# A two-layer decoder: layer norms from sums of the writing operation, squares on ScalarE, centred memory values, and a new order of the steps

## The chip, the cores and the metric

The kernel runs on one core of one Trainium2 chip. The metric is the time of one execution on the device in microseconds (us). One launch computes everything; the four sequences of the batch are worked off one after another, two at a time in flight.

## The reference, cut to what matters

Four sequences of 512 tokens with 256 channels, in float32, go through six sublayers. Each is added to its input and followed by a layer norm without weights:

```
x = LN(x + causal_attention(x))
x = LN(x + cross_attention(x, ctx, mask))   # its output goes through a norm of its own, gamma, beta
x = LN(x + sign_ffn(x))                     # three dense layers, weights +1 / -1
x = LN(x + performer(x))                    # linear attention, 16 heads, relu features
x = LN(x + mlstm(x, ctx, ctx))              # 8 heads, gated scores, norm of each head's 32 channels
x = LN(x + quantized_ffn(x))                # rounded tokens and weights, convolution, silu
```

The matrix LSTM of the fifth line, for each head: `H = (C @ v) / (max(|sum C|, exp(-m)) + 1e-6)`, then `(H - mean(H)) / sqrt(var(H) + 1e-5)` over the 32 channels of the head. `C` are scores times a decay, `v` the head's columns of ctx.

## The kernel before, in words

A sequence is worked on in two halves. The **front half** (names self, cross, sign, perf) holds the first four sublayers, the **back half** (first, mlstm, quant) the norm behind the performer and the last two. The back half of sequence b runs beside the front half of sequence b+1; the front half of sequence 0 and the back half of sequence 3 have nothing beside them. Each half has four PSUM banks, used in turn; a bank's next matmul waits until its last content was read.

Tokens lie on partitions in four tiles of 128, t = 0 to 3; "p" is a pair of tiles. There is no loop over engines: each engine has one queue in order, and its program for a half is a list of named steps (`yield "cross.score0"`). `weave` (L340) merges the lists of both halves, and of the preparation of weights (`prep`), by a table of due times (`FRONT_TIMES`, `BACK_TIMES`, `PREP_TIMES`, one column for each engine). The times decide nothing but the order in each queue: the step that is due first comes next, and an engine waits for every operand of it before it looks at the one behind.

The steps that matter here:

- **A layer norm** is `stats` (VectorE, L1351: `bn_stats` for each of two tiles, `bn_aggr` for each, one small addition), `rstd` (GpSimd, a power of -0.5), and `normalize` (VectorE makes the shift and tile 2p, ScalarE makes tile 2p+1). TensorE then turns the pair (`to_channels`, L806 to L812). There are six for a sequence and a seventh within the cross attention (`cross.in_`): 14 pairs for each sequence.
- **keep_clock** (L800) is a row of idle 128x512 matmuls that only keep TensorE busy: in front of `mlstm.cols` six of them (12 for the last sequence), and some in the performer and in the last half.
- **mlstm**: `gate`, `logf`, `csum`, `g`, `high`, `nmd`, `part2`, `part3` make the gates on VectorE one after another; `softplus`, `negated`, `part1` are ScalarE's share; `raw0`, `raw1` are the scores; `cols` turns the gates into columns, behind which GpSimd weighs the keys; `head0` to `head7` make the decay (matmul, exp on ScalarE, product on VectorE); then `out0` to `out3`. For each out tile VectorE does `ratio` and `square` (denominator in four small operations, the quotient L1758, its mean L1763, its centring L1765, gn_w L1769), ScalarE the squares (L2137), VectorE `var`, GpSimd a power (`pow`, L2276), VectorE `scale` (L1786, L1790).
- **quant**: `q0` to `q7` on VectorE (L1887, L1880) and ScalarE make the rounded hidden tiles; `down0` to `down3` (L1317) need all eight.
- **prep** on ScalarE for the sign layers: `w10` to `w17` (L1937), `w2` (L1940), and `abs00` to `abs13` (L1948).

## Time and profile before

| | |
|---|---|
| median of 3 runs (lowest to highest) | 945.58 us (940.68 to 945.62) |
| the profiled execution's own time | 945.73 us |
| its span, first to last instruction | 944.5 us |
| TensorE matmul busy | 773.9 us, 82% |
| VectorE busy | 605.1 us, 64% |
| ScalarE busy | 368.3 us, 39% |
| GpSimd busy | 148.0 us, 16% |
| mean granted TensorE clock | 0.939 of full speed |

A busy share is a mean over the whole span. What a change is worth is read from the stretch in which it lies and from what the engine that ends there waited for. DMA moved 26 GB/s in the mean and its queues took 8% of their engines' time.

### The profile page before, as it was taken

Reading aid. Unit: us, or ns where it says so; the run is one execution under the profiler, and the core shown is the slowest. Engines: PE = TensorE matmul, PEld = TensorE weight load, DVE = VectorE, ACT = ScalarE, POOL = GpSimd, SP = SyncE. Lnnn points to the kernel's source line nnn. Section 1 sums busy time; section 2 is a strip of 40 time slices with the busy share of each in tenths; the row PEclk is TensorE's granted clock in tenths of the full one; section 3 lists DMA queues with packets and bytes.
Section 4 is the critical chain, followed back from the end, with each engine's and each line's share of the span. In section 5 each row is a group of like instructions: output and inputs, shape, how many; then the busy total and the mean of one; then the engine's idle time right before and its main releaser. Section 6 shows DMA issues by size and latency. Waiting matters only on the chain.

```text
span 944.5 us, 14796 instructions
## 1 busy us (share of the span) xinstructions
PE 773.9 (82%) x5907; PEld 515.7 (55%) x5954; DVE 605.1 (64%) x1485; ACT 368.3 (39%) x654; POOL 148.0 (16%) x236
## 2 busy tenths in 40 slices
PE   8787977889999887799999877899999878656244
PEld 5554545666765545666765555666755456335112
DVE  1544643336866768647876688647767697448686
ACT  2473121224632156335531265246522364242072
POOL 4010020011311300011502200011412100103200
PEclk9898999999979999999999999999999999869568
DMA  9310000020010000020010000100100000000000
GB/s 361 140 45 1 1 1 24 2 67 23 2 45 1 1 23 2 2 89 23 2 45 1 1 24 2 37 31 1 46 1 1 0 2 1 23 1 1 0 1 23
DMA packets 13508, 25.86 MB, mean 27 GB/s; under 512 B 768, under 2 KB 7040, under 8 KB 13184
## 3 DMA queue, kind: packets, MB, share of 16 engines
q1 hardware_dynamic: 13440, 24.92, 7.5%
q8 instruction: 47, 0.77, 0.3%
q14 instruction: 21, 0.17, 0.1%
HBM read 22.82 MB, written 2.10 MB: 26 GB/s over the span
## 4 chain that ended last, share of the span: by engine, by line
PE 60%; DVE 24%; ACT 9%; issue 4%; another core or an unknown queue 1%; POOL 1%; DVEq 0%; ACTq 0%
PE bank L972 12%; PE bank L818 7%; PE bank L826 5%; PE bank L866 3%; PE bank L982 3%; PE bank L1067 3%; PE bank L1253 3%; PE bank L960 3%; DVE work L1714 2%; PE bank L849 2%; PE bank L804 2%; DVE work L1631 2%; PE bank L1015 2%; DVE work L1846 1%; PE bank L1049 1%
## 5 line engine op out<-in xcount | busy, mean ns | idle before, releaser
L2203 POOL TENSOR_TENSOR rstd<-rstd,minus_half 128x2 f32<-128x2 f32 x56 | 43.3, 775 | 460.3 <-DVE rstd L1362 460.3
L972 PE MATMUL bank<-work,f0w 128*128 128x512 f16 x512 | 111.7, 379 | 0.0
L972 PEld LDWEIGHTS bank<-work,f0w 128*128 128x128 f16 x512 | 50.2, 98 | 59.6
L2041 ACT ACTIVATE work<-bank 128x512 f16<-128x512 f32 x64 | 37.7, 595 | 106.9 <-PE bank L972 80.9
L804 PE MATMUL bank<-bar_upper,identb 128*128 128x512 bf16 x119 | 38.2, 441 | 43.4 <-DVE x L1371 12.7
L1550 DVE SCALAR_TENSOR_TENSOR work<-bank,work 128x512 f16<-128x512 f32 x64 | 42.2, 687 | 32.7 <-ACT work L2041 32.7
L1434 DVE TENSOR_REDUCE small<-bank 128x1 f32<-128x512 f32 (+3 forms) x32 | 18.6, 582 | 65.8 <-PE bank L850 47.1
L866 PE MATMUL bank<-work 128*128 128x256 f32 x208 | 50.5, 387 | 3.6 <-ACT work L1979 3.6
L804 PEld LDWEIGHTS bank<-bar_upper,identb 128*128 128x128 bf16 x138 | 13.6, 108 | 62.4 <-issue 20.1
L2079 ACT ACTIVATE work<-bank 128x512 f32<-128x512 f32 x32 | 18.9, 592 | 67.6 <-PE bank L1067 67.6
L2276 POOL TENSOR_TENSOR small<-small,minus_half 128x8 f32<-128x8 f32 x16 | 26.2, 1638 | 116.7 <-DVE small L1777 116.7
L866 PEld LDWEIGHTS bank<-work 128*128 128x128 f32 x208 | 38.4, 191 | 9.5 <-issue 4.0
L1067 PE MATMUL bank<-work 64*128 64x128 f32 x512 | 38.1, 289 | 5.6 <-issue 4.0
L1631 DVE TENSOR_TENSOR work<-bank,upper 128x512 f32<-128x512 f32 x32 | 22.1, 690 | 29.2 <-PE bank L1067 28.7
L1714 DVE TENSOR_TENSOR work<-work 128x512 f32<-128x512 f32 x32 | 27.5, 899 | 16.6 <-ACT work L2127 16.5
L818 PE MATMUL bank<-xT,perf_w 128*128 128x512 f32 x64 | 32.3, 639 | 6.4 <-ACT work L2066 5.3
L1356 DVE BATCH_NORM_STATS2 stats<-y 128x6 f32<-128x256 f32 x96 | 36.1, 415 | 1.9 <-ACT y L2019 1.9
L1253 PE MATMUL bank<-work 128*128 128x66 f32 (+1 forms) x256 | 32.8, 286 | 4.4 <-DVE work L1714 4.4
L1067 PEld LDWEIGHTS bank<-work 64*128 64x128 f32 x512 | 31.9, 191 | 8.2 <-issue 6.8
L1253 PEld LDWEIGHTS bank<-work 128*128 128x128 f32 x256 | 32.5, 206 | 5.2 <-issue 5.2
L1957 ACT ACTIVATE work<-bank,small 128x512 f32<-128x512 f32 (+3 forms) x32 | 19.4, 605 | 34.2 <-DVE small L1434 34.2
L849 PE MATMUL bank<-work 128*128 128x512 f32 x64 | 30.1, 593 | 0.2
(271 smaller groups left out, 1766.1 us busy)
## 6 DMA issues: line engine op xcount, KB each, us to landing
ctxT<-in_ctxT SPq DMA_DIRECT2D x8, 512.0 KB, 4.8
work<-in_mask SPq DMA_DIRECT2D x4, 1024.0 KB, 5.7
xT<-in_xT SPq DMA_DIRECT2D x4, 512.0 KB, 3.6
work<-in_w SPq DMA_DIRECT2D x1, 2048.0 KB, 18.9
ctx<-in_ctx SPq DMA_DIRECT2D x4, 512.0 KB, 3.9
out<-y SPq DMA_DIRECT2D x4, 512.0 KB, 3.1
perf_w<-in_perf_w SPq DMA_DIRECT2D x1, 1536.0 KB, 15.9
x<-in_x SPq DMA_DIRECT2D x2, 512.0 KB, 7.1
```

Source lines behind the costliest of these rows:

```text
L804: nc.tensor.matmul(u.bank[:, :], identb[:, :], bar_upper[:, :, :].rearrange("p a b -> p (a b)"), start=True, stop=True)
L818: ins = nc.tensor.matmul(u.bank[:, :], weights[:, k, c0:c0 + P], src[:, k, :], start=(k == 0), stop=(k == NC - 1))
L826: ins = nc.tensor.matmul(u.bank[:, j * C:(j + 1) * C], src[:, k, t * P:(t + 1) * P], weights[:, k, c0:c0 + C], start=(k == 0), stop=(k == ...
L849: nc.tensor.matmul(u.bank[:, 0:n], a_qT[:, k, t * P:(t + 1) * P], keys[:, k, 0:n], start=(k == 0), stop=False)
L866: ins = nc.tensor.matmul(u.bank[:, 0:C], probT[:, t % 2, j * P:(j + 1) * P], v[:, j, :], start=(j == 0), stop=(j == n - 1))
L972: ins = nc.tensor.matmul(u.bank[:, :], f0w1[:, k, m * P:(m + 1) * P], h1[part][:, k, :], start=(k == 0 and part == 0), stop=(k == NF - 1 a ...
L1067: ins = nc.tensor.matmul(u.bank[:, here], kf[rows, pair, here], qf[rows, pair, here], start=(i == 0), stop=True, tile_position=(PM * i, 0) ...
L1253: ins = nc.tensor.matmul(u.bank[:, h * LV1:(h + more) * LV1], cT[:, h, t * P:(t + 1) * P], values_[:, h * LV1:(h + more) * LV1], start=Tru ...
L1550: low_part(what, m, dst, number + m, lambda o, x, hi: nc.vector.scalar_tensor_tensor(out=o, in0=x, scalar=0.0, in1=hi, op0=ALU.max, op1=AL ...
L1631: nc.vector.tensor_tensor(inner[:, r % 4, :].rearrange("p (t q) -> p t q", t=NT), u.bank[:, :].rearrange("p (t q) -> p t q", t=NT), upper[ ...
L1714: nc.vector.tensor_tensor(cT[:, h, :], cT[:, h, :], decay[h % 2], ALU.mult).then_inc(decayed.sem, 1)
L2203: nc.gpsimd.tensor_tensor(s.rstd[:, two], s.rstd[:, two], minus_half[:, 0:2], ALU.pow).then_inc(s.rstd_made.sem, 1)
```

## The change

It has five parts.

1. **Sums.** `bn_stats` and `bn_aggr` go. The operation that writes a tile in front of a norm now has `accum_out=...sums`. For the residual adds behind the performer this makes one 128x512 addition into two of 128x256.
2. **Squares.** ScalarE has a new step `squares` for each pair and norm, under the old name `stats`: two activations with an accumulated output. VectorE's `stats` shrinks to one small operation that waits for them, and `normalize` waits for its own shift.

```diff
-        def stats(s, b, i, src, ready, p, name):
+        def stats(s, b, i, p, name):
             yield f"{name}stats{p}"
-            for t in (2 * p, 2 * p + 1):
-                if ready[t]:
-                    dve.wait_ge(*ready[t])
-                m = vec.mark(nc.vector.bn_stats(s.stats[:, t, :], src[:, t, :]))
-            dve.wait_ge(*m)
-            for t in (2 * p, 2 * p + 1):
-                m = vec.mark(nc.vector.bn_aggr(s.mv[:, t, :], s.stats[:, t, :]))
-            dve.wait_ge(*m)
             two = slice(2 * p, 2 * p + 2)
-            nc.vector.tensor_scalar(s.rstd[:, two], s.mv[:, two, 1], EPS, None, ALU.add).then_inc(s.var_in.sem, 1)
+            dve.wait_ge(*s.squared.at(b, s.place[i, p]))
+            nc.vector.tensor_scalar(s.rstd[:, two], s.squares[:, two], 1.0 / C ** 3, EPS, ALU.mult,
+                                    ALU.add).then_inc(s.var_in.sem, 1)
...
+        def squares(s, b, i, src, spare, ready, p, name):
+            yield f"{name}stats{p}"
+            for t in (2 * p, 2 * p + 1):
+                act.wait_ge(*ready[t])
+                ins = nc.scalar.activation(spare[:, t, 0:C], src[:, t, :], ACT.Square, bias=s.sums[:, t:t + 1], scale=-float(C),
+                                           accum_out=s.squares[:, t:t + 1])
+            ins.then_inc(s.squared.sem, 1)
```

3. **Centred memory values.** Once for each sequence VectorE subtracts from ctx the mean of each head (`mlstm.centre`, two operations over 128x1024, between `mlstm.xT1` and `mlstm.gate`); GpSimd's four copies go. The head's output then has mean zero, so the mean and the centring of each out tile go, and the quotient too: the denominator's square times 1e-5 takes the place of the 1e-5 in the variance. ScalarE squares the undivided tile.

```diff
-                m = vec.mark(nc.vector.tensor_scalar(l_den, l_den, 1e-6, None, ALU.add))
+                m = vec.mark(nc.vector.tensor_scalar(l_den, l_den, 1e-6, 1e18, ALU.add, ALU.min))
                 dve.wait_ge(*m)
-                m = vec.mark(nc.vector.reciprocal(l_rden, l_den))
...
-                m = vec.mark(nc.vector.tensor_tensor(back.y[:, t, :]..., tmp[:, :, 0:LD], l_rden..., ALU.mult))
-                yield f"mlstm.square{t}"
...
-                m = vec.mark(nc.vector.tensor_reduce(mean[:, g], y_groups[:, g, :], AX, ALU.add))
-                dve.wait_ge(*m)
-                nc.vector.scalar_tensor_tensor(out=y_groups[:, g, :], in0=mean[:, g]..., scalar=-1.0 / LD, ...)
-                weighed[t] = vec.mark(nc.vector.tensor_tensor(rest[:, t % 2, C:2 * C], back.y[:, t, :], gn_w, ALU.mult))
+                vec.mark(nc.vector.scalar_tensor_tensor(out=den2[...], in0=l_den, scalar=EPS, in1=l_den, op0=ALU.mult, op1=ALU.mult))
+                weighed[t] = vec.mark(nc.vector.tensor_tensor(rest[...], tmp[:, :, 0:LD], gn_w..., ALU.mult))
```

(The dots inside a line stand for slices.) The scratch tile `tmp` becomes two, used in turn.

4. **Columns of the gates.** On TensorE and ScalarE `mlstm.cols` and `mlstm.weigh` move from in front of `head0` to in front of `head2`. The six idle matmuls there go; the last sequence keeps 11, in front of `head0` and in a bank of the front half:

```diff
+            if b == B - 1:
+                pe.wait_ge(*gates_final.at(b))
+                keep_clock(fb["perf", b, "out", 1], 11, False)
             for h in range(LH):
+                if h == 2:
+                    yield from columns_of_gates()
```

5. **New due times.** Merged by `weave`, they give these queues (F is the front half, B the back half of the sequence before it; only what changes and matters):

- TensorE before: F self.q to cross.xT0; B xT0, xT1; F q0, xT1; B raw0; F q1 to cross.product3; B raw1, cols, head0 to head3; F sign.xT0; B rest of the heads and states; ... F sign.c0 to perf.xT1; B quant.turn0; F perf.qk.0, v1; B row1, turn1; F fq.0, q.1; B hidden0 to hidden4; F fk.0, ft.0, state.0; B hidden5, 6; F score0.0; B hidden7; F ... fk.1; B topT; F ft.1; B row2; F state.1 to den0.1; B down0 to down3; F num0.1 and on.
- TensorE after: F self.q; B xT0; F self.v to self.score2; B xT1 and gate; F to self.product1; B raw0; F to self.product3; B raw1; F cross.xT0 to cross.score0; B head0, head1, cols, head2; F score1, score2, product0; B head3 to head7 with two states; F to cross.product3; B state3, out0, out1; F sign.xT0; B out2; F sign.early, xT1; B out3; F sign.a0 to b6; B quant.turn0; F b7, c0, c1, c2; B row1, turn1, hidden0 to hidden4; F c3, perf.xT0, v0, xT1, qk.0; B hidden5 to hidden7; F v1, fq.0 to num0.0; B topT; F score2.0; B row2; F score3.0 to ft.1; B down0 to down3; F state.1 and on.
- VectorE after, around the performer: ... F perf.fk.1; B q5, q6, q7, down0, down1, down2, stats0; F ft.1; B norm0, down3; F state.1. Before, q4 to q6 stood behind state.1 and score0.1, and ft.1 in front of q0.
- ScalarE after, from self: score3 to product2, self.stats0, B raw0, self.norm0, self.product3, self.stats1, cross.xT0, self.norm1, B negated, part1, F cross.q0, q1, B part3, raw1, head0, head1, weigh, F cross.score0. B softplus stands in front of self.score3 (before: behind cross.q0).
- ScalarE in the first sequence, before: w10, w11 behind self.product1; w12 to w14 behind self.product2; w15 to w17 and w2 behind cross.q0; abs00 to abs13 behind cross.score1. After: w10 to w17 and w2 all behind cross.q0, in front of cross.q1 and cross.score0; abs00 to abs13 behind cross.score2, in front of cross.product0 and score3. VectorE's `prep.scales`, for which they wait, moves from behind self.stats0 to behind cross.xT1.
- VectorE in the last half is unchanged but for parts 1 to 3 and `stats`, `norm` of mlstm, which go behind `var`. In the last front half ScalarE's quant.norm1 of the sequence before and VectorE's share of it come before the performer's output.

## Rows read from the trace of the kernel before

**Rows 1.** Windows: length, PE, PEld, DVE, ACT, POOL busy, clock, DMA share, GB/s.

```profile
400.70:606.10 205.40, 182.14 (x1461) 123.25 (x1472) 146.80 (x359) 87.28 (x156) 34.64 (x54) 0.99 0.07 21
...
811.60:944.50 132.90, 64.10 (x390) 40.09 (x393) 86.57 (x204) 46.24 (x71) 22.16 (x34) 0.72 0.03 8
```

**Rows 2.** TensorE's waits, 400.7 to 606.1 us: total, times, longest.

```profile
PE bank L1253 <- DVE work L1714: 1.7, 1, 1.7
PE bank L804 <- ACT work L2100: 1.5, 1, 1.5
```

**Rows 3.** Timeline of TensorE, 519 to 609 us: start, length, [idle before].

```profile
524.71 1.99 PE L826 MATMUL bank<-perf_w,xT 128*128 128x256 f32 x8 [0.67 <-ACT xT L1921]
...
579.44 0.95 PE L1029 MATMUL bank<-perf_w,work 32*128 32x128 f32 x24
...
582.27 2.76 PE L1049 MATMUL bank<-work 128*128 128x68 f32 x24
```

**Rows 4.** Chain that ended last, 811 to 944.5 us: start, length.

```profile
813.71 1.29 DVE x L1653 x2
...
820.51 1.10 PE bank L811 x4
...
839.14 0.61 ACT work L2100
...
840.26 4.11 PE bank L804 x11
...
847.29 0.54 PE bank L1213
...
857.90 1.96 PE bank L1253 x16
...
861.20 0.43 DVE y L1758
...
862.11 0.43 DVE y L1765
...
890.62 0.41 DVE x L1371
```

**Rows 5.** Groups of instructions: busy, mean ns | idle before.

```profile
L1356 DVE BATCH_NORM_STATS2 stats<-y 128x6 f32<-128x256 f32 x96 | 36.1, 415 | 1.9 <-ACT y L2019 1.9
...
L2276 POOL TENSOR_TENSOR small<-small,minus_half 128x8 f32<-128x8 f32 x16 | 26.2, 1638 | 116.7 <-DVE small L1777 116.7
...
L1887 DVE TENSOR_TENSOR work<-work,bank 128x512 f32<-128x512 f32 x32 | 21.2, 683 | 2.5 <-PE bank L1260 2.5
...
L1359 DVE BATCH_NORM_AGGREGATE mv<-stats 128x2 f32<-128x6 f32 x112 | 13.9, 166 | 1.9
...
L1880 DVE TENSOR_SCALAR work<-work 128x512 bf16<-128x512 f32 x32 | 13.2, 424 | 0.1
...
L2137 ACT ACTIVATE work<-y 128x256 f32<-128x256 f32 x16 | 6.6, 414 | 36.5 <-DVE y L1765 36.5
...
L1957 ACT ACTIVATION_READ_ACCUMULATOR work<-bank,small 128x1 f32 x32 | 6.1, 192 | 0.0
...
L2094 ACT ACT_TABLE_LOAD x4 | 5.1, 1283 | 0.1
...
L1948 ACT ACTIVATE f1w<-work 128x512 bf16<-128x512 f32 x8 | 4.9, 615 | 0.0
...
L1937 ACT ACTIVATE f0w<-xT,signed 128x1024 f16<-128x1024 uint8 x4 | 4.7, 1234 | 3.9 <-DVE signed L1387 3.9
```

**Rows 6.** Timeline of all engines, 8 to 90 us.

```profile
36.79 2.69 PE L866 MATMUL bank<-work 128*128 128x256 f32 x8 [3.59 <-ACT work L1979]
...
47.08 0.69 DVE L1348 COPY xT<-bank 128x512 f32<-128x512 f32 x1 [3.29 <-PE bank L811]
```

**Rows 7.** Timeline of TensorE, 54 to 87 us.

```profile
55.37 0.60 PE L857 MATMUL bank<-ident,work 128*128 128x128 f32 x4
...
72.34 1.09 PE L811 MATMUL bank<-ident,x 128*128 128x128 f32 x4 [3.18 <-DVE x L1371]
```

More of the change, by code:

```diff
@@ new lines @@
+    ("self.product3", 197, 236, 257, None),
+    ("self.stats0", None, 236, 212, None),
+    ("self.norm0", None, 236, 257, None),
+    ("self.stats1", None, 260, 263, None),
+    ("self.norm1", None, 261, 273, None),
+    ("cross.xT0", 264, None, 263, None),
+    ("cross.bar0", None, 282, None, None),
+    ("cross.xT1", 291, 285, None, None),
+    ("cross.bar1", None, 285, None, None),
+    ("cross.bar2", None, 285, None, None),
+    ("cross.bar3", None, 285, None, None),
+    ("cross.q0", 291, None, 295, None),
@@ new lines @@
+    ("cross.add0", None, 489, None, None),
+    ("cross.stats0", None, 489, 499, None),
+    ("cross.in_stats1", None, 516, 499, None),
+    ("cross.norm0", None, 520, 499, None),
+    ("cross.stats1", None, 536, 499, None),
+    ("cross.in_norm1", None, 516, None, None),
+    ("sign.xT0", 520, 536, 519, None),
+    ("cross.norm1", None, 536, 519, None),
+    ("cross.add1", None, 521, None, None),
+    ("cross.in_rstd0", None, None, None, 556),
+    ("cross.rstd0", None, None, None, 556),
+    ("cross.in_rstd1", None, None, None, 556),
@@ L1466, in front_half @@
         def front_half(b):
-            self_read = [fb["self", b, "product", t].read for t in range(NT)]
             def self_product(t):
@@ L1664, in back_half @@
             for p in range(2):
-                yield from stats(back, b, 0, back.x, [fb["perf", b, "out", t // 2].read for t in range(NT)], p, "first.")
+                yield from stats(back, b, 0, p, "first.")
+            for p in range(2):
                 yield from normalize(back, b, 0, back.x, back.x, p, "first.")
@@ L1995, in front_half @@
                                u.bank[:, :].rearrange("p (j c) -> p j c", j=2)).then_inc(u.emptied, 1)
+            self_read = [fb["self", b, "product", t].read for t in range(NT)]
             def self_product(t):
+                if t >= 2:
+                    yield from squares(front, b, 0, front.y, fx[b % 2], self_read, t - 2, "self.")
                 if t == 3:
@@ L2086, in back_half @@
             for p in range(2):
+                yield from squares(back, b, 0, back.x, cT, [fb["perf", b, "out", t // 2].read for t in range(NT)], p, "first.")
+            for p in range(2):
                 yield from normalize(back, b, 0, back.x, back.x, p, "first.")
```

755 lines of the change are left out of this document (384 added, 371 removed).

## The prediction

> **What bounds the kernel now.** I read the windows by batch first, then TensorE's waits in a middle batch, its timeline there, the chain of the last 133 us, and the timeline of the first 90. In a middle batch TensorE is busy 182.1 of 205.4 us, at a clock of 0.99; VectorE 146.8, ScalarE 87.3 [rows 1]. So TensorE sets the pace for some 680 us. Its 23 us of idle time are short waits, few above 1.5 us: 1.7 for the last heads, 1.5 for a bank in front of the idle matmuls [rows 2], 0.67 for a copy in front of the performer's values, one of three such waits there [rows 3]. They are latencies of in-order queues, so less VectorE work gives back nothing of the 182; only waits and TensorE's own instructions count. The last 132.9 us are the last back half, alone: VectorE 86.6 busy, TensorE 64.1 with idle matmuls in it, clock 0.72 [rows 1]. The chain walks there from VectorE to GpSimd and back; a microsecond less of VectorE work is one less of time. The first 90 us are a third regime: ScalarE's preparation stands in the same queue as the attention's exponentials.
>
> **VectorE and ScalarE totals.** The statistics that go are 36.1 + 13.9 us in these two groups [rows 5], and as many per tile for the rest. New on ScalarE are 112 squares. The nearest row is the square of 128x256 at 0.41 us, and an accumulator read behind an exponential is 0.19 [rows 5]: 0.6 us each, 67 us in all, on an engine that is 43% busy in a middle batch. Hidden by that slack where nothing waits; where something does, it is placed below. VectorE's accumulated outputs (96) have no row. Bounds: nothing, or ScalarE's read of 0.19 each, 18 us over the run. I take 0.06, the gap kind of cost; in the last half some 8 lie on the chain, so 0.5 us, at most 1.5. The Trainium skill (VectorE: DVE Perf Modes, "Two Vector instructions with no wait between them") says that an operation with accumulator output is two instructions, the second a read; no run here shows it yet, and it would speak for the upper bound.
>
> **The last half, in its order.**
> - First norm. The residual adds now start when the last ScalarE norm is written, at 813.71, and TensorE turns the second pair at 820.51 [rows 4]. After the change that norm is finished during the performer, which gives 0.7 us or more; two squares (1.2) replace statistics of about 1.0 plus a separate chain for each pair, since both pairs now run ahead. I walk it to 818.1: -2.4.
> - Centring: two operations over 128x1024, four times the length of those at 0.43 [rows 4], so 2.6 us, during the gate matmuls and in front of nothing: 0 here. If that cover were gone, +2.6.
> - Gates. The idle matmuls start at 840.26 behind ScalarE's score copies from 839.14 and take 4.11, the columns take until 847.29, and only then comes head 0 [rows 4]. Now the idle matmuls start about 5 us sooner, in another bank, head 0 at about 839.8, the columns behind head 1. Head 2 is then limited by the same 3 us of columns, and is done at about 846.7, where it was 850.7; the products on VectorE follow at 0.9 each: -4 (bounds -2 and -5, by when the clock rises).
> - Out tiles. From 857.90 to 890.62 [rows 4]. Each tile loses quotient, mean and centring at 0.43 (two of the three shown) and a 0.21 reciprocal and gains 0.17: -1.4 with the gaps, four times -5.6. GpSimd's power of 1.64 [rows 5] is now less covered: I walk idle gaps of 1.7 at three of the four powers, as now, and norm 1 behind squares that ScalarE does while VectorE works on the next tile. The walk ends 5.7 us sooner.
> - The end: squares of 0.6 against statistics of 0.4 for the last tile, +0.2.
> Sum: -11.9, plus 0.5 for accumulators: about -11.5; bounds -14 and -9.
>
> **The first batch.** Now TensorE waits 3.59 us at 36.79 for a copy that stands behind two weight conversions [rows 6]. That goes, and with it the slow clock behind it: the second copy of cross.xT, at 47.08 [rows 6], comes 4.8 us sooner, at 42.3. But then ScalarE does w10 to w17 and w2 in one piece: 8 x 1.23 [rows 5] less overlap, 9.4, and 2.2 for w2: 11.6 us, begun only when prep.scales is done behind that copy. Then come the q1 copies (0.84) and the first exponential (0.9). The first turned score is possible 14 us behind the copy, at about 57.1; it is 55.37 now [rows 7]. Behind it, eight `abs` of 0.62 + 0.19 [rows 5] stand in front of the exponential of score 3 as well: some 3 us more. The cross norm's chain has two pairs of squares on ScalarE in front of sign.xT0, at 72.34 now [rows 7]: +1.5. Together +6; bounds +2 (fast clock kept until the burst) and +9 (slow clock behind two long waits). What was hidden under TensorE work is late here, and no later batch gives it back.
>
> **A middle batch (three of them).** Gone: six idle matmuls at 0.215, 1.3 us, and their bank's wait of 1.5 and the wait of 1.7 for the last product [rows 2]: -4.5. VectorE has 6 us less between fq.0 and spread.0, which should take that part's waits back to those of the first batch: -1.1.
> Added, each by walking the queues:
> - Only self.q (3.4 us) covers the chain from the performer's output to B xT0: +0.4. raw1 waits for raw0's copies behind self.stats0 (+1.2), q0 for the copy behind self.stats1 (+0.7), score0 for q copies that stand behind part1, which waits for VectorE's `high` (+1.1), head 0 for raw1's copies (+0.9), and xT1's wait (+0.9): +5.2.
> - sign.c to fq.0: VectorE has conv and hidden steps between c2, norm0, c3 and norm1: waits of 5.5 instead of 2.4, so +3.1.
> - down. From ft.1 at 579.44 to state.1 at 582.27 it is 2.8 us [rows 3]. After, ft.1's drain on VectorE stands behind q5 to q7 at 0.68 + 0.42 each [rows 5], the last downs and `stats0`, which waits for squares: state.1 waits about 3.5 instead of 1.1: +2.4.
> All of them at once give +5.1 for a batch, none of them -5.6. A wait eats the backlog that makes the next one, so the walk overstates the sum; the two ends are equally far, and I take 0, that is, half of the added waits. Three batches: 0, bounds -17 and +15.
> The moved softplus changes tables twice between self scores, 1.28 each [rows 5], as before behind cross.q0; the walk has its exponential ready when TensorE wants it. The Trainium skill (ScalarE: Activation LUTs, "Table sets: the hidden batching unit") gives about 2.7 us for a load. By that, 2.8 more would lie there for each batch; the row decides.
> SyncE's loads follow ctx and xT uses that come earlier or hardly move: 0.
>
> **Sum.** -11.5 + 6 + 0 = -5.5; with rounding of the walk I say -6: 945.7 - 6, 939.5. The profiled execution's 945.73 is 0.15 above the median, which changes nothing.
>
> **The rivals.**
> 1. The middle batches take all added waits (+15): 945.7 - 11.5 + 6 + 15 = 955. For it: each wait is in the order of the queues. Against: VectorE has some 15 us less to do in a batch. It decides from +1.9 for a batch on. This is the one on the slower side.
> 2. None of them comes: 945.7 - 11.5 + 6 - 17 = 923. For it: less VectorE work shortens the queues behind which all of them stand.
> 3. The first batch keeps its fast clock and the middle gains a little (-2 each): 945.7 - 11.5 + 2 - 6 = 930.
> 4. The squares lengthen the last half's chain: each accumulator read 0.19, the centring uncovered: the last half gains only 7 and the whole comes to 944. No gain, though the work is gone.
>
> **How the numbers follow.** This kernel's runs differ by up to 0.5%, 4.7 us; that is what a measurement can tell. Forecast 0.3, rival 1 0.28, rival 2 0.12, rival 3 0.2, rival 4 0.1. The forecast's own range is 934 to 945. From 2 and 3, and most of the forecast, faster by over 0.5% comes to 0.5; the rest of the forecast, 4 and the near end of rival 1 give within 0.5% 0.22; rival 1 leaves 0.28. The range that leaves out two in ten goes from 922 to 956.
>
> **What would show it.** Last half: 121 to 122 us from the performer's end, head 0 some 7 us sooner, out tiles 27 us. First batch: a TensorE wait of 5 us or more in front of the first cross turn, sign.xT0 at 77 or later. Middle: period 205, waits in front of state.1, perf.v0 and score0. Wrong if a middle batch differs by more than 3 us from 205, or if ScalarE's burst finds TensorE with other work.

## The result and the profile after

The changed kernel takes 944.92 us in the median of 20 runs (942.86 to 947.70), the kernel before 940.65 in 20 runs beside it (933.03 to 945.86). The ratio is 1.0053, with a 95% interval of 1.0029 to 1.0077: slower by half a per cent. The forecast was 939.5, with a chance of 0.5 for a gain of over 0.5% and 0.28 for a loss of over 0.5%. 944.92 lies inside its range of 922 to 956, but on the other side of no change.

Both executions are cut at the same place, the start of the performer's projection (the 16 passes over `perf_w,y`), because everything behind the last of them is the last half alone. The columns are length, busy time of PE, PEld, DVE, ACT and POOL with the number of instructions, granted clock, DMA share and GB/s. First the windows of the kernel before; the first one begins with TensorE's first projection.

```profile
9.46:191.93 182.47, 151.12 (x1115) 97.11 (x1124) 77.69 (x198) 59.89 (x115) 15.24 (x24) 0.93 0.16 59
191.93:400.69 208.76, 185.50 (x1462) 126.42 (x1473) 144.65 (x349) 84.91 (x153) 33.96 (x53) 0.98 0.06 19
400.69:606.14 205.45, 182.16 (x1462) 123.27 (x1473) 146.85 (x359) 87.28 (x156) 34.64 (x54) 0.99 0.07 21
606.14:810.14 204.00, 182.03 (x1462) 123.66 (x1473) 145.59 (x359) 87.51 (x156) 34.59 (x54) 0.99 0.04 14
810.14:944.50 134.36, 65.56 (x395) 41.40 (x400) 88.00 (x209) 46.84 (x72) 22.16 (x34) 0.73 0.02 8
```

The same windows of the changed kernel:

```profile
7.95:195.75 187.80, 150.63 (x1116) 96.44 (x1125) 72.69 (x180) 68.44 (x151) 17.07 (x27) 0.94 0.16 61
195.75:408.02 212.27, 184.38 (x1454) 123.28 (x1466) 131.95 (x319) 100.10 (x215) 34.75 (x50) 0.98 0.06 18
408.02:615.97 207.95, 180.01 (x1454) 121.76 (x1466) 132.01 (x319) 101.38 (x216) 34.76 (x50) 1.00 0.06 21
615.97:823.91 207.94, 180.01 (x1454) 121.84 (x1467) 131.94 (x319) 101.38 (x216) 34.74 (x50) 1.00 0.04 14
823.91:945.80 121.89, 70.56 (x394) 48.30 (x399) 76.78 (x179) 52.09 (x94) 19.68 (x29) 0.71 0.03 9
```

Three things are to be seen. The last part fell from 134.36 to 121.89 us: -12.5. The performer's projection of the first batch starts at 195.75 instead of 191.93: +3.8. Each middle batch grew, by 3.51, 2.50 and 3.94: together +10.0. The sum is the 1.3 us between the two spans (944.5 and 945.8). In the columns of DVE and PE, VectorE lost 13 to 15 us of work per middle batch and TensorE 1 to 2, and the batch is still longer. So what grew is TensorE's idle time, from 22.0 us (204.00 - 182.03) to 27.9 (207.94 - 180.01).

The waits of TensorE that make it up stand in its timeline (start, length, in brackets the idle time before and what ended it). The changed kernel, one middle batch:

```profile
442.36 1.17 PE L1180 MATMUL bank<-xT,ctxT 32*128 32x128 f32 x32 [0.68 <-ACT work L2151]
...
444.79 1.99 PE L930 MATMUL bank<-xT,cross_w 128*128 128x256 f32 x8 [0.68 <-ACT xT L1943]
...
448.35 1.97 PE L930 MATMUL bank<-xT,cross_w 128*128 128x256 f32 x8 [1.13 <-DVE xT L1362]
451.33 1.96 PE L855 MATMUL bank<-work 128*128 128x512 f32 x4 [1.01 <-ACT work L2048]
455.00 0.38 PE L1226 MATMUL bank<-parts,head_row 128*128 128x512 bf16 x1 [1.72 <-ACT work L2151]
...
537.13 0.63 PE L817 MATMUL bank<-ident,x 128*128 128x128 f32 x4 [0.70 <-DVE x L1380]
...
542.34 3.70 PE L824 MATMUL bank<-xT,perf_w 128*128 128x512 f32 x8 [1.37 <-DVE xT L1362]
...
550.31 1.14 PE L1021 MATMUL bank<-work,perf_w 32*128 32x512 f32 x8 [1.24 <-DVE work L1577]
...
583.76 1.14 PE L1021 MATMUL bank<-work,perf_w 32*128 32x512 f32 x8 [1.62 <-DVE y L1653]
```

The first five are those that the forecast walked: raw1 (0.68), q0 (0.68), the second xT (1.13), score0 (1.01) and head 0 (1.72), 5.2 us together. The forecast had 5.2 too (with 0.4 behind self.q), but not term by term: 1.2 for raw1 and 0.9 for head 0. None of them stood there before; there the same stretch had 1.46 in front of the idle matmuls and 1.69 in front of the last heads' product [rows 2]. The other four lines are waits in front of perf.xT0 (0.70), perf.qk.0 (1.37), fq.0 (1.24) and, late in the batch, fq.1 (1.62). From sign.c up to fq.0 the waits add up to 4.9 us where the batch before has 2.4; up to ft.0 to 7.0 where it has 3.8.

The new instructions, as groups (busy, mean ns, idle before), in the changed kernel:

```profile
L1952 ACT ACTIVATE x<-y,sums 128x256 f32<-128x256 f32 x56 | 28.0, 501 | 26.8 <-DVE y L1812 12.9 <-DVE y L1566 7.3 <-DVE y L1923 5.5
L1952 ACT ACTIVATION_READ_ACCUMULATOR x<-y,sums 128x1 f32 x56 | 10.5, 188 | 0.0
...
L1923 DVE DVE_READ_ACCUMULATOR y<-bank,small,x 128x1 f32 x16 | 1.3, 83 | 0.0
...
L1691 DVE SCALAR_TENSOR_TENSOR work<-small,ctx 128x1024 f32<-128x1024 f32 x4 | 4.9, 1225 | 0.1
```

A square costs 0.50 and its read 0.19, 0.69 us (forecast 0.6), 77 us in 112 of them. VectorE's accumulated output is a second instruction that takes 0.083 us, not the 0.19 of ScalarE's: 8 us in 96 of them. That it is a second one the Trainium skill says (VectorE: DVE Perf Modes, "Two Vector instructions with no wait between them"), and this trace agrees. The last line is the second operation of the centring, 1.23 us for each sequence. Table loads stayed 16 at 1.283 us each, and the exponential behind the load at 433.01 starts at 434.30, 0.01 us behind its end. The Trainium skill (ScalarE: Activation LUTs, "Table sets: the hidden batching unit") gives about 2.7 us for a load; the trace does not agree, and the row was the one to go by.

### The profile page after: what moved, and what is told of

Read it like the earlier page. It is cut to its first block, busy times and chain, and to the rows that moved or that the text cites. A ratio compares the mean times of both kernels' runs of the same rounds, so it can differ in the third digit from the quotient of the medians.

```text
span 945.8 us, 14839 instructions
## 1 busy us (share of the span) xinstructions
PE 771.6 (82%) x5885; PEld 514.9 (54%) x5935; DVE 547.7 (58%) x1333; ACT 425.3 (45%) x894; POOL 147.3 (16%) x220
## 4 chain that ended last, share of the span: by engine, by line
PE 64%; DVE 19%; ACT 9%; issue 5%; POOL 2%; ACTq 0%; POOLq 0%; DVEq 0%
PE bank L978 12%; PE bank L824 5%; PE bank L832 5%; PE bank L855 4%; PE bank L872 4%; PE bank L1073 3%; PE bank L1267 3%; PE bank L966 2%; PE bank L1055 2%; PE bank L988 2%; PE bank L1021 2%; POOL rstd L2258 2%; DVE work L1639 1%; DVE work L1863 1%; DVE work L1869 1%
## 5 line engine op out<-in xcount | busy, mean ns | idle before, releaser
L1558 DVE SCALAR_TENSOR_TENSOR work<-bank,work 128x512 f16<-128x512 f32 x64 | 41.8, 687 | 36.0 <-ACT work L2087 35.7
L810 PE MATMUL bank<-bar_upper,identb 128*128 128x512 bf16 x103 | 34.5, 454 | 32.1 <-DVE work L1872 11.1
L2128 ACT ACTIVATE work<-bank 128x512 f32<-128x512 f32 x32 | 19.1, 596 | 76.3 <-PE bank L1073 76.3
L872 PEld LDWEIGHTS bank<-work 128*128 128x128 f32 x208 | 39.2, 196 | 6.1 <-ACT work L2011 1.0
L824 PE MATMUL bank<-xT,perf_w 128*128 128x512 f32 x64 | 32.0, 634 | 10.2 <-ACT work L2115 5.1
L810 PEld LDWEIGHTS bank<-bar_upper,identb 128*128 128x128 bf16 x119 | 11.6, 110 | 52.4 <-ACT work L2115 12.8
L1952 ACT ACTIVATE x<-y,sums 128x256 f32<-128x256 f32 x56 | 28.0, 501 | 26.8 <-DVE y L1812 12.9
L1267 PE MATMUL bank<-work 128*128 128x66 f32 (+1 forms) x256 | 34.9, 297 | 1.2 <-DVE work L1739 1.2
L1267 PEld LDWEIGHTS bank<-work 128*128 128x128 f32 x256 | 35.0, 219 | 1.4 <-issue 1.4
L855 PE MATMUL bank<-work 128*128 128x512 f32 x64 | 32.3, 629 | 3.2 <-ACT work L2048 3.0
L2115 ACT ACTIVATE work<-bank 128x512 f32<-128x512 f32 x40 | 21.3, 596 | 24.6 <-PE bank L1021 24.6
```

Source lines behind the costliest of these rows:

```text
L810: nc.tensor.matmul(u.bank[:, :], identb[:, :], bar_upper[:, :, :].rearrange("p a b -> p (a b)"), start=True, stop=True)
L824: ins = nc.tensor.matmul(u.bank[:, :], weights[:, k, c0:c0 + P], src[:, k, :], start=(k == 0), stop=(k == NC - 1))
L855: nc.tensor.matmul(u.bank[:, 0:n], a_qT[:, k, t * P:(t + 1) * P], keys[:, k, 0:n], start=(k == 0), stop=False)
L872: ins = nc.tensor.matmul(u.bank[:, 0:C], probT[:, t % 2, j * P:(j + 1) * P], v[:, j, :], start=(j == 0), stop=(j == n - 1))
L1267: ins = nc.tensor.matmul(u.bank[:, h * LV1:(h + more) * LV1], cT[:, h, t * P:(t + 1) * P], values_[:, h * LV1:(h + more) * LV1], start=Tru ...
L1558: low_part(what, m, dst, number + m, lambda o, x, hi: nc.vector.scalar_tensor_tensor(out=o, in0=x, scalar=0.0, in1=hi, op0=ALU.max, op1=AL ...
```

## The experiments

All were compared by their wholes (timed, against the kernel before on the same chip) and by the same five parts of one profiled execution: start of the performer's projection in the first batch ("first"), the three middle batches, and the last part. The runs were timed in groups, each with the kernel before beside it, whose medians were 937.45 (e1 to e4), 939.86 (e5 to e8), 936.56 (e9 to e12) and 937.44 us (e13 to e16); so the ratios are compared, and not the medians.

| run | median us | ratio to before, 95% | first | middle batches | last |
|---|---|---|---|---|---|
| before | 940.65 | | 191.9 | 208.8, 205.5, 204.0 | 134.4 |
| changed | 944.92 | 1.0053 (1.0029 to 1.0077) | 195.8 | 212.3, 208.0, 207.9 | 121.9 |
| e1 | 957.23 | 1.0215 (1.0165 to 1.0266) | 188.2 | 218.7, 213.1, 218.1 | 120.5 |
| e2 | 945.15 | 1.0088 (1.0055 to 1.0120) | 190.5 | 212.3, 207.9, 208.0 | 121.9 |
| e3 | 939.65 | 1.0023 (0.9990 to 1.0056) | 192.9 | 209.3, 207.5, 209.1 | 120.7 |
| e4 | 970.53 | 1.0350 (1.0306 to 1.0394) | 196.1 | 220.4, 216.7, 215.0 | 118.9 |
| e5 | 945.79 (one run) | | 192.0 | 208.8, 205.5, 204.0 | 134.3 |
| e6 | 944.57 | 1.0048 (1.0011 to 1.0084) | 195.8 | 212.3, 207.9, 208.0 | 121.9 |
| e7 | 930.74 | 0.9923 (0.9885 to 0.9961) | 185.4 | 206.8, 205.1, 205.2 | 124.0 |
| e8 | 940.18 | 1.0024 (0.9993 to 1.0055) | 186.1 | 207.5, 207.3, 205.8 | 130.9 |
| e9 | 936.73 | 0.9982 (0.9948 to 1.0016) | 187.3 | 209.9, 207.3, 215.5 | 116.9 |
| e10 | 954.16 | 1.0154 (1.0113 to 1.0195) | 195.9 | 211.8, 211.7, 211.7 | 120.7 |
| e11 | 957.97 | 1.0198 (1.0158 to 1.0237) | 190.5 | 215.8, 214.1, 215.8 | 120.4 |
| e12 | 934.50 | 0.9972 (0.9935 to 1.0009) | 185.2 | 203.1, 204.5, 204.5 | 132.2 |
| e13 | 942.37 | 1.0045 (1.0003 to 1.0086) | 190.1 | 208.7, 205.4, 204.0 | 133.5 |
| e14 | 943.61 | 1.0075 (1.0047 to 1.0103) | 189.8 | 208.8, 205.5, 204.0 | 134.4 |
| e15 | 950.19 | 1.0151 (1.0112 to 1.0190) | 198.6 | 212.3, 208.0, 207.9 | 121.9 |
| e16 | 929.27 | 0.9937 (0.9904 to 0.9970) | 185.0 | 206.8, 205.1, 207.6 | 123.1 |

**e1, the new code in the old order.** All of the changed code, merged by the due times of the kernel before; a few examples of the rows:

```diff
-    ("mlstm.raw1", 181, None, 319, None),
+    ("mlstm.raw1", 296, None, 318, None),
-    ("quant.q5", None, 1393, 1493, None),
+    ("quant.q5", None, 1341, 1332, None),
-PERIOD, LATER = 4961, 50
+PERIOD, LATER = 3914, 160
```

> All the changed code (sums from the writing operations, squares on ScalarE, centred memory values, columns behind head 1), but merged by the due times of the kernel before; the new steps stand beside the ones that they belong to. Theory A, the order: the 3 us that each middle batch lost (2.5 to 3.9, by the starts of the performer's projection) come from the new order of the queues. Then a middle batch takes 203 to 205.5 us here, the projection of the first starts by 192.5 (195.75 in the changed kernel), the last half stays at about 122, and the whole is 927 to 934. Theory B, the squares: 0.69 us each on ScalarE stand in front of copies that TensorE waits for, in any order. Then a middle batch still takes 207 to 209, and the whole is 938 to 945.

Both theories of this run fell. The performer's projection of the first batch and the last part came as theory A had them (188.2 and 120.5), but the middle batches became 5 to 10 us longer still. The window of the second one, in e1:

```profile
406.90:619.95 213.05, 186.32 (x1467) 125.33 (x1467) 131.57 (x320) 101.76 (x216) 33.08 (x50) 0.98 0.06 21
```

So the new order didn't cause the loss by itself; without it the new code is worse. Most of the difference is clock. The traces of the kernel before and of the changed one each lack some ten of TensorE's matmul records in such a batch; e2's trace, with the same matmuls as the changed kernel, has them, so it is the one to compare with:

```profile
402.80:610.74 207.94, 181.90 (x1466) 121.76 (x1466) 132.00 (x319) 101.31 (x216) 34.70 (x50) 1.00 0.07 21
```

Of the 5.1 us by which e1's batch is longer, 4.4 are busy time at a clock of 0.98 in place of 1.00 and 0.7 idle time. The last middle batch, at a clock of 0.95, is 10.2 us longer than e2's, of which 9.9 are busy time.

**e2, the old place of the preparation** in the changed kernel (and `self.score4` to `self.norm0` of VectorE at 238 instead of 236, so that the scales and two conversions of VectorE, w00 and w01, can stand in front of them):

```diff
-    ("prep.w10", None, None, 370, None),
+    ("prep.w10", None, None, 106, None),
-    ("prep.w12", None, None, 370, None),
+    ("prep.w12", None, None, 273, None),
-    ("prep.scales", None, 390, None, None),
+    ("prep.scales", None, 297, None, None),
```

> The changed kernel, with ScalarE's w10 to w17 and VectorE's scales placed as in the kernel before (w10, w11 behind self.product1, w12 to w14 behind self.product2, the rest behind cross.q0). If the conversions in one piece cost the first batch its time, as forecast, the 7.32 us wait in front of the first cross turn shrinks to below 4 us and the projection starts 2 to 4 us sooner, at 192 to 194 instead of 195.75; the eight abs in front of score 3 stay. If the squares cost it, the start stays within 0.5 of 195.75. Middle batches and the last half unchanged under either, so the whole is 942 to 944 or 946.

The projection starts at 190.5, 5.2 us sooner, more than the 2 to 4 that were expected. The changed kernel's own timeline of the first batch has these waits of TensorE:

```profile
51.97 1.11 PE L863 MATMUL bank<-ident,work 128*128 128x128 f32 x4 [7.32 <-ACT work L1989]
64.87 0.63 PE L863 MATMUL bank<-ident,work 128*128 128x128 f32 x4 [2.40 <-ACT work L1989]
74.22 0.63 PE L817 MATMUL bank<-ident,x 128*128 128x128 f32 x4 [3.57 <-DVE x L1380]
```

and in e2 the first of them has become two others, of 2.46 and 2.87, while the one behind the `abs` is unchanged:

```profile
34.97 1.97 PE L872 MATMUL bank<-work 128*128 128x256 f32 x8 [2.46 <-ACT work L2011]
39.80 0.59 PE L817 MATMUL bank<-ident,x 128*128 128x128 f32 x2 [2.87 <-issue]
...
53.11 0.66 PE L863 MATMUL bank<-ident,work 128*128 128x128 f32 x4 [0.28 <-ACT work L1989]
64.37 0.63 PE L863 MATMUL bank<-ident,work 128*128 128x128 f32 x4 [2.40 <-ACT work L1989]
```

That the conversions in one piece cost the first batch its time is shown for the profiled execution. In the timed runs the gain doesn't appear (945.15 against 944.57 in e6); why is not settled.

**e3, no squares**, the changed order:

```diff
-                ins = nc.scalar.activation(spare[:, t, 0:C], src[:, t, :], ACT.Square, bias=s.sums[:, t:t + 1], scale=-float(C),
-                                           accum_out=s.squares[:, t:t + 1])
+                ins = nc.scalar.activation(s.squares[:, t:t + 1], src[:, t, 0:1], ACT.Copy, bias=float(C) ** 3, scale=0.0)
```

> The changed kernel with each of the 112 squares replaced by one element per partition set to a constant (the variances are left out; the waits and the places in the queues stay). Theory A, the order: middle batches stay at 206.5 to 208, the last half loses 3 to 5 us of squares on its chain, the whole 936 to 942. Theory B, the squares: middle batches fall to 204 to 205.5, the whole is 929 to 934.

A middle batch at full clock takes 207.50 us, 0.45 less than with the squares, although ScalarE has 10 us less to do:

```profile
402.20:609.70 207.50, 181.80 (x1466) 121.87 (x1467) 131.50 (x319) 91.19 (x188) 34.67 (x50) 1.00 0.07 21
```

In this order the squares cost a middle batch at full clock next to nothing; what they cost the last part is 1.2 us. The rest of the 6.3 us between the two profiles lies in the first batch (192.9 against 195.8) and in the first middle batch (209.3 against 212.3, at clocks of 0.99 and 0.98), and the last middle batch is 1.2 longer without them. Theory B wanted 204 to 205.5 for all three; it falls, for this order.

**e4, the statistics on VectorE again**, the changed order, centring and columns as changed. In `stats` (and without the `accum_out` and ScalarE's `squares`):

```diff
+            for t in (2 * p, 2 * p + 1):
+                dve.wait_ge(*ready(t))
+                m = vec.mark(nc.vector.bn_stats(s.stats[:, t, :], src[:, t, :]))
...
-            nc.vector.tensor_scalar(s.rstd[:, two], s.squares[:, two], 1.0 / C ** 3, EPS, ALU.mult,
-                                    ALU.add).then_inc(s.var_in.sem, 1)
+            nc.vector.tensor_scalar(s.rstd[:, two], s.mv[:, two, 1], EPS, None, ALU.add).then_inc(s.var_in.sem, 1)
```

> The changed kernel with sums and squares undone: statistics and aggregates on VectorE again, no accumulated outputs, no squares; order, centring and columns as changed. Theory A, the order: middle batches take 207 to 210 (VectorE has 14 us more again), the last half 123 to 126, the whole 945 to 955. Theory B, the squares: middle batches fall to 205 or less and the whole to 940 or less.

215 to 220 us for a middle batch, more than the upper end of theory A: the new order relies on the lighter VectorE. Here too it is mostly the clock:

```profile
416.56:633.30 216.74, 189.41 (x1466) 126.22 (x1467) 144.63 (x349) 86.97 (x156) 35.00 (x50) 0.96 0.06 20
```

Against e2's batch 7.5 us more of busy time and 1.3 of idle time. The last part is 118.9, below the 123 to 126 that theory A had: with the statistics on VectorE it is 3.0 us shorter than with sums and squares (at clocks of 0.77 and 0.71).

**e5 and e6, both kernels once more.**

> The kernel before, unchanged, for a second profile. Its 20 timed runs spread from 933 to 946 us, and the one profile is at the upper end. Theory: the spread is stretches at the lower level of TensorE's clock. If so, a profile nearer to 935 shows fewer of them at the same work: a middle batch without one takes 203.5 to 204.5 us, and the last 134.4 us (from the projection's start) hold part of the rest. Rival: the spread is in transfers or waits at the same clock, and the middle batches take 204 to 209 again with the clock at 0.99.

> The changed kernel, unchanged, for a second profile and for timing beside the others of this group. By the same theory: middle batches of 208 us at full clock (4 more than in the kernel before), a last stretch of about 122, 943 to 947 in all.

e5 came back at 945.79 us with every part within 0.06 us of the first profile, so it told nothing of the other runs. The timed runs do: each comes with its mean granted clock, and the 23 runs of the kernel before beside e1 go from 933.0 us at 0.951 to 945.4 us at 0.939. A difference of 0.012 over 940 us is 11 us of full clock, nearly the whole 12.4. (The changed kernel's 20 runs spread less, 942.9 to 947.7.) The second profile of the changed kernel repeats the first within 0.1 us.

**e7, centring and columns alone**, in the old order, with VectorE's statistics. (e7, e8 and e4 keep two small things of the change beside: the residual additions behind the performer in two, and a norm that waits for its own shift.) Against the kernel before, the centring is this (on GpSimd only the ones stay; `ratio`, `square` and `var` as in the change):

```diff
+            yield "mlstm.centre"
...
+            m = vec.mark(nc.vector.tensor_reduce(v_mean, heads, AX, ALU.add))
+            dve.wait_ge(*m)
+            nc.vector.scalar_tensor_tensor(out=l_v1[:, :, :, 0:LD].rearrange("p t h d -> p (t h) d"),
+                                           in0=v_mean.unsqueeze(2).broadcast_to([P, G, LD]), scalar=-1.0 / LD, in1=heads,
+                                           op0=ALU.mult, op1=ALU.add).then_inc(memory_v.sem, 1)
```

> The kernel before with its own order and times, its statistics on VectorE, and only two parts of the change: the memory values centred once (with the second tmp and what goes with it) and the gate columns behind head 1 without the middle batches' six idle matmuls. Theory A (the middle was lost to the order that the squares needed, the tail was won by centring and columns): middle batches at 203 to 205.5, the last stretch at 123 to 126, the whole 922 to 930. Rival: the squares and accumulated sums gave the last half its gain; then the last stretch stays at 129 or more and the whole at 932 or more.

The middle and the last part fall as theory A had them; the whole is 930.74 us, just above its 922 to 930. It is faster than both kernels:

```profile
597.31:802.51 205.20, 180.97 (x1455) 123.13 (x1466) 143.12 (x350) 87.42 (x156) 32.47 (x50) 0.99 0.05 14
802.51:926.50 123.99, 65.56 (x394) 41.34 (x399) 84.31 (x201) 46.73 (x72) 20.89 (x30) 0.73 0.03 9
```

10.4 of the 12.5 us that the change won in the last part are here, without one square. Its first batch ends at 185.4, 6.5 us before that of the kernel before, though neither of the two parts has a step there; that is taken up under "The base" below.

**e8, centring alone, and e12, columns alone.** e8 is e7 with `columns_of_gates()` in front of head 0 and `keep_clock(u, 12 if b == B - 1 else 6)` in their bank; e12 is the kernel before with

```diff
-            keep_clock(u, 12 if b == B - 1 else 6)
...
+            if b == B - 1:
+                pe.wait_ge(*gates_final.at(b))
+                keep_clock(fb["perf", b, "out", 1], 11, False)
             for h in range(LH):
+                if h == 2:
+                    yield from columns_of_gates()
```

> As the one before, but with the columns in front of head 0 again and the idle matmuls in their bank. Theory: the out tiles' share of the gain, 5 to 7 us of the last stretch, stays, and the 3 to 5 us of the columns go: 926 to 934 in all. Middle batches at 203.5 to 205.5.

> The kernel before with one part alone: the gate columns behind head 1, the idle matmuls gone from the middle batches and moved to the projection's bank in the last half. With centring and columns together the last stretch fell from 134.3 to 124.0 us, with centring alone to 130.9. Theory: the two add up, so the last stretch is 126.5 to 128.5 here. Rival: the columns' gain is a matter of the clock's stretches and needs the shorter out tiles; then it is 130 or more. Middle batches 203 to 206, the whole 930 to 938.

Neither alone gives what both give: -3.5 and -2.2 in the last part, -10.4 together, so the theory of e12 (126.5 to 128.5) fell, and its rival's 130 or more came. Cut at the first out tile and at the turn of the quantiser's input, the last part shows where. From the projection to the first out tile takes 47.8 us before, 47.8 in e8, 43.5 in e12, 41.0 in e7 and 38.7 in the changed kernel. From there to the turn takes 35.7, 30.2, 35.7, 30.1 and 31.1. From the turn on it is 50.9 before and 52.1 to 53.1 in the other four, where nothing was taken out. So centring is worth 5.5 us at the out tiles with either place of the columns, the columns' part 4.3 us in front of them without centring and 6.8 with it, and 1 to 2 are given back behind, in each run once. That 4.3 became 6.8 goes with the clock, as that rival has it (0.69 over the last part in e8 and e12, 0.73 in e7); that it is the cause is not shown.

What the columns' part does there is to be seen in TensorE's timeline. In e8 the idle matmuls wait for the bank that ScalarE's score copies empty, and the columns come behind:

```profile
829.31 2.09 PE L1180 MATMUL bank<-xT,ctxT 32*128 32x128 f32 x32 [4.33 <-ACT work L2129]
836.30 3.83 PE L810 MATMUL bank<-bar_upper,identb 128*128 128x512 bf16 x11 [4.91 <-ACT work L2129]
...
840.07 0.44 PE L1198 MATMUL bank<-small,ones 8*128 8x72 f32 x2
```

In the changed kernel they fill that wait:

```profile
842.25 2.09 PE L1180 MATMUL bank<-xT,ctxT 32*128 32x128 f32 x32 [4.33 <-ACT work L2151]
844.67 3.59 PE L810 MATMUL bank<-bar_upper,identb 128*128 128x512 bf16 x10 [0.34 <-issue]
848.78 0.39 PE L1226 MATMUL bank<-parts,head_row 128*128 128x512 bf16 x1 [0.52 <-ACT work L2151]
```

In the middle batches e12 has no idle matmuls and yet, behind the first one, only 1 us less in one batch (204.48 against 205.45) and 0.5 more in the next (204.49 against 204.00). Its timeline says why: the two waits of [rows 2] stand there as before, 1.38 now directly in front of the heads, and 2.16 in front of the product.

```profile
446.16 0.39 PE L1222 MATMUL bank<-head_row,parts 128*128 128x128 bf16 x4 [1.38 <-ACT work L2107]
...
461.27 2.59 PE L1260 MATMUL bank<-work 128*128 128x66 f32 x16 [2.16 <-DVE work L1721]
```

**e9, the old order without squares** (e1 with the edit of e3).

> The changed code in the old order, with each square replaced by one constant per partition (the variances are left out). In that order, with the squares, the middle batches took 218.7, 213.1 and 218.1 us. Theory C: the squares' time on ScalarE is what the old order does not bear. Then the middle batches fall to 204 to 207 here and the whole to 930 to 938. Rival: the sums' way over ScalarE costs by its waits (VectorE stands in its queue until ScalarE has come to its step), whatever a square takes; then the middle batches stay at 210 or more.

Theory C (204 to 207) and its rival (210 or more) both miss in two of the three batches: 218.7 and 213.1 became 209.9 and 207.3, nearer to C. The last one stayed at 215.5, at a clock of 0.95. A middle batch at full clock:

```profile
397.24:604.56 207.32, 180.03 (x1455) 122.02 (x1466) 132.31 (x320) 91.41 (x188) 33.02 (x50) 1.00 0.07 21
```

27.3 us idle, 3 more than in e7 (24.2), which has the same order and the statistics on VectorE. So the rival is right too for some 3 us: the way of the sums over ScalarE costs its waits even when a square takes nothing.

**e10, the columns in front of head 0**, idle matmuls as changed:

```diff
+            yield from columns_of_gates()
             for h in range(LH):
-                if h == 2:
-                    yield from columns_of_gates()
```

> The changed kernel with the gate columns in front of head 0 again (and ScalarE's weigh in front of its first head), idle matmuls as changed: none in the middle, 11 in the last half. Forecast's reading of the last half: the columns behind head 1 gave 3 us there, so the last stretch goes from 121.9 to 124 to 126. In the middle the 1.7 us wait in front of the heads is filled by the columns: 206 to 207.5 for a batch instead of 207.9. Rival: the gain of the last half came from the idle matmuls' earlier place alone; then it stays within 1 us of 121.9. Whole: 940 to 947.

The last part is 120.7, not 124 to 126. The rival is right: the place of the columns gave nothing there; the idle matmuls' place did. In the middle, the forecast of this run (206 to 207.5) was wrong by 4 to 6 us. The columns wait 2.24 for VectorE's gate rows at 455.17, against 1.72 for the heads in the changed kernel, and the clock, 1.00 in the four microseconds before, is 0.57 from 458 to 462; it is 0.79 once more, from 552 to 560:

```profile
407.68:619.35 211.67, 183.24 (x1454) 123.33 (x1466) 131.87 (x319) 101.54 (x216) 34.71 (x50) 0.98 0.07 21
```

Of the 3.7 us that the batch grew by, 3.2 are busy time at a lower clock (183.24 against 180.01).

**e11, sign.c3 sooner**, with the preparation of e2:

```diff
-    ("sign.c3", 1040, 992, None, None),
+    ("sign.c3", 1008, 992, None, None),
```

> The changed kernel with TensorE's sign.c3 directly behind sign.c2 (it stood behind row1, turn1 and hidden0 to hidden4), and the preparation placed as in the kernel before. If a middle batch lost 3.2 us between sign.c and fq.0 because VectorE's norms stand behind c3, the waits of 0.70 and 0.78 in front of perf.xT0 and perf.v0 go and a middle batch takes 206 to 207 instead of 207.9. Rival: the waits only move; 207.5 to 208.5. The first batch ends at 190.5 as in the second run; the whole 935 to 942.

The rival, and worse than it: the wait of 0.70 became one of 2.45, since VectorE stood no sooner at its norm (the turn comes 130.8 us into the batch, 129.1 in the changed kernel). The batch has a clock of 0.96 in place of 1.00, with 0.82 and 0.84 from 535 to 545 and 0.60, 0.50 and 0.88 from 585 to 600:

```profile
537.05 0.63 PE L817 MATMUL bank<-ident,x 128*128 128x128 f32 x4 [2.45 <-DVE x L1380]
```

```profile
406.21:620.29 214.08, 186.41 (x1454) 125.51 (x1466) 132.08 (x319) 101.52 (x216) 34.69 (x50) 0.96 0.07 21
```

(the first fence is e11's timeline of TensorE, the second its window). The batch is 6.1 us longer and has 6.4 us more of busy time.

**e13, e14 and e15, another start**: `range(2)` and `range(5)` for the `range(3)` of idle matmuls over `ones` at TensorE's very start, in the kernel before, and `range(5)` in the changed one.

> The kernel before with two instead of three idle matmuls over ones at its very start; nothing else. Theory: the forecast's base was off because the kernel before spreads from 933 to 946 us by where its work falls in the stretches of half clock, and the profiled execution was at the slow end (23.9 us at half clock in the first batch, 10.2 in the second). Then a start moved by a microsecond gives other stretches in an otherwise equal stream: the first batch ends anywhere from 185 to 192 and the second takes 203.5 to 209, while waits before the first fall of the clock stay the same to 0.1. Rival: the 945.7 us belong to the stream itself; then all four batch times come back within 0.5 us.

> The same with five of them, so that TensorE's first real work starts some 1.5 us later or finds the clock otherwise. Same theories and same numbers; this and the one before should differ from each other too if the stretches decide.

> The changed kernel with five idle matmuls at the start. By the theory that waits, not stretches of half clock, made its middle batches longer, the third and fourth batch take 207.5 to 208.5 us again (they had no half clock); only the first two and the last half may move, by up to 6 us together. If the 208 were luck of the clock, one of them falls to 205 or less.

The middle batches come back to 0.03 us in all three, as the rival of e13 and e14 has it. What moved is the first batch's end and, in e13, the last part by 0.8. From TensorE's first projection on, the first batch of e13 takes 182.4 us as before (182.5), that of e14 179.7, at a clock of 0.96 in place of 0.93: there the theory, not the rival, has it. The timed runs of e14 are 0.75% above the kernel before, and those of e15 some 5 us above the changed kernel, more than a later start explains (0.7 and 3.1 us in the profiles); that is open. For the changed kernel, e15 means that 207.9 is no luck of one profile.

**e16, e7 once more.**

> The kernel with centring and columns alone once more, to be timed in other rounds: 0.985 to 0.997 of the kernel before, 926 to 936 us.

929.27 us and 0.9937 (0.9904 to 0.9970), as expected. Its profile doesn't repeat that of e7 everywhere, though the kernel is the same: the last middle batch took 207.6 at a clock of 0.98, 205.2 at 0.99 in e7, and the last part 123.1 for 124.0.

## Why the prediction was wrong

**The last half: right by sum, in its steps only in part.** -11.5 was forecast (-14 to -9), -12.5 measured. Out tiles -4.6 (forecast -5.7; -5.5 in e7 and e8). Up to the first out tile -9.0, where the first norm and the gates together had -6.4. The turn of the second pair comes 2.8 sooner (forecast 2.4), the gate matmuls 3.3. The rest is the idle matmuls filling the 4.9 us wait. The forecast named that and the columns' move in one breath; e10 shows that the second was worth nothing. Behind the turn +1.2 instead of +0.7 with accumulators.

**The first batch: the mechanism right, the sum in part by luck.** +6 was forecast (+2 to +9), +3.8 measured, +5.3 from TensorE's first projection on; the other 1.5 us is an earlier start, 7.95 instead of 9.46. It stands in front of everything that the change touches: the idle matmuls at the very start took 4.32 us instead of 5.49. TensorE waits 7.32 us in front of the first cross turn (forecast at least 5) and 2.40 in front of score 3 (some 3). But that turn comes at 51.97, where the walk had 57.1, and sign.xT0 at 74.22, not at 77 or later; 1.9 us more were lost behind it, where the forecast had nothing. And the 182.5 us to compare with are those of an execution whose clock was low in this batch (see "The base").

**The middle batches: the step that failed.** "A wait eats the backlog that makes the next one, so the walk overstates the sum ... I take 0, that is, half of the added waits." The ends were -5.6 and +5.1; measured are +3.5, +2.5 and +3.9. In the batch whose waits are shown above, 10.7 us were booked as added and 9.2 came: those of the front half's attention with 5.2 of 5.2, sign.c to fq.0 with 2.4 of 3.1, ft.1 to state.1 with 1.0 of 2.4, and 0.5 in a sign layer that the walk didn't have. What was booked as gone came too, 6.5 of 5.6: 2.1 of busy time, 3.5 of waits in front of the idle matmuls, the product and a turn, 0.9 net in the rest of the performer. Together +2.7, against 2.5 by the windows. By this account the added waits were not halved: no backlog in front of TensorE, which was the bound, ate them. So it was rival 1, priced at +15, that came with +10.0, over its mark of +1.9 in each batch: 945.7 - 12.5 + 3.8 + 10.0 = 947.0, and the profiled execution took 947.10. By the forecast's own sign (over 3 us from 205) the first of the three was wrong, and the other two came to 2.9.

**Why these waits exist at all** is the part that the forecast didn't see. It took the new order as a given list of gains and losses. e1, e4 and e7 show that order and code are a pair. A middle batch takes 213 to 219 us for new code in the old order, 215 to 220 for the old statistics in the new order, 212 and twice 208 for new code in the new order, and for the old statistics in the old order, with centring and columns (e7, e16), 205 to 208, mostly 205. The sums' way over ScalarE takes 13 to 15 us from VectorE, which wasn't the bound of a middle batch, and puts a ScalarE step with its waits in front of each norm. The new order repairs most of that (213.1 to 207.9 in the second middle batch, 4.4 us of it clock), not all. Which waits cost which clock is not shown. e3 excludes the squares' duration as the cause in the new order (0.45 us); in the old order it matters (e9).

**The base.** "The profiled execution's 945.73 is 0.15 above the median, which changes nothing" was the second step that failed. It was the median of three runs, and 20 have 940.65; those three spread over 4.9 us, the 20 over 12.8. By profiles the change costs 1.3 us, by the timed runs' ratio 0.5%, 5 us; the gap is the kernel before's runs at a higher clock. e12 shows where they can lie. Its first batch has the same steps as the kernel before (VectorE x198, ScalarE x115 in both windows), and yet takes 176.8 us, not 182.5; its first middle batch takes 203.1, not 208.8:

```profile
8.37:185.16 176.79, 146.43 (x1116) 93.50 (x1125) 77.67 (x198) 59.93 (x115) 16.05 (x26) 0.97 0.17 64
...
185.16:388.24 203.08, 180.90 (x1455) 123.37 (x1466) 143.27 (x349) 84.74 (x153) 33.11 (x53) 0.99 0.06 19
```

With the earlier start that is 12.5 us, nearly as much as the kernel before's runs spread. e7 has such a first batch too (176.9). In both the clock is 1.00 from 44 to 52 us, where the kernel before has 0.53. Against such a first batch the changed one's 187.8 us is +11, not +5.3. That the kernel before's faster runs are of this kind is likely and not shown, since no profile caught one: e5, e13 and e14 came back to the same middle batches. What decides it is open.

## What to carry to other kernels

Here one engine was the bound of the middle batches: 13 to 15 us less work for another gave nothing, and new waits in the bound engine's in-order queue came with most of their length (8.7 of the 10.7 us booked, and 0.5 that was not booked). Walk the waits and book them whole. Take a change of several parts apart by regimes: here two parts that pay in the last half (0.992 and 0.994 of the kernel before, in two timings of both without the rest) were carried together with one that costs in each middle batch. An order tuned for one code is tuned for that code only: neither may be judged without the other, and a local repair of one wait (e10, e11) made middle batches up to 3.7 and 7.8 us longer.

## What the runs showed of the hardware that was not expected

VectorE's accumulator read takes 0.083 us where ScalarE's takes 0.19. The time of the idle stretch isn't the whole price of a wait: in e10 0.5 us more of wait in one place went with 3.2 us more of busy time, in e11 1.75 us with 6.4, at mean clocks of 0.98 and 0.96 in place of 1.00; the changed kernel's own waits of 1.72 and 1.62 left the clock at 1.00 through two batches. A second profile can repeat the first to a few hundredths of a microsecond in a batch (208.76, 208.77, 208.74 and 208.75 in the kernel before, e5, e13 and e14), while the timed runs of the kernel before spread over 1.4%; and it can differ by 2.4 us in one batch (e7 and e16, the same kernel). One profile, however exactly it repeats, is not the median.
